# Attention moved to the end of the scan, wide products throughout, and the turn between batches written out by hand, in a fused Mamba and transformer kernel on one core

## The reference

```python
# 1. selective scan over ctx (512 x 256), gated by the normalised x
u = silu(causal_conv4(in_proj @ ctx.T) + conv_b)          # 512 channels x 512 tokens
dt = softplus(dt_proj @ (x_proj[:16] @ u) + dt_b);  Bm, Cm = x_proj[16:] @ u
state = state * exp(dt * A) + dt * u * Bm                  # 16 states per channel
y = sum_n(state[n] * Cm[n]) + D * u
x = x + tanh(g0) * (y * silu(layernorm(x))).T
# 2. feed-forward with weights rounded to -1, 0, 1 and activations rounded to 8 bits
x = x + tanh(f0) * bitlinear(gelu(bitlinear(layernorm(x), w1)), w2)
# 3. attention over features: energies of ctx, applied to the normalised x
x = x + tanh(g1) * layernorm(x) @ softmax(q(ctx) @ k(ctx).T).T
# 4. ordinary feed-forward in float32, 512 -> 2048 -> 512
x = x + tanh(f1) * (gelu(layernorm(x) @ p1.T + b1) @ p2.T + b2)
```

## Time and profile before

| | |
|---|---|
| device time, median of 3 runs | 1057.2 us (1055.8 to 1058.83) |
| the profiled execution | 1057.6 us, its span 1055.8 us |
| busy share of the span | PE 78%, DVE 78%, ACT 63%, POOL 53% |
| granted TensorE clock, mean | 0.896 |
| chain that ended last, by engine | PE 27%, DVE 21%, issue 17%, ACT 13%, DMA 9%, POOL 8% |
| the same scans of the last two loop passes | start at 601.42 and 833.70 us |
| closing part begins on TensorE | 911.52 us |

### The profile page before, as it was taken

One profiled execution on the slowest core, in us unless ns is written; L12 is line 12 of the kernel. 1 busy time (PEld: TensorE's weight loads), 2 busy tenths in 40 slices (PEclk: granted clock), 3 DMA queues, 4 the chain that ended last, 5 costly groups with the idle time before them and its releaser, 6 DMA issues.

```text
span 1055.8 us, 10904 instructions
## 1 busy us (share of the span) xinstructions
PE 823.3 (78%) x2704; PEld 399.7 (38%) x2704; DVE 824.9 (78%) x1001; ACT 665.5 (63%) x972; POOL 564.1 (53%) x493
## 2 busy tenths in 40 slices
PE   5442320699699987989699988889799988898998
PEld 2110110344334334444334334344333434445887
DVE  4879968887988897687998898777998897764333
ACT  4679969366589962365589962565599852533442
POOL 0398785123997783123997783134997782133000
PEclk9555555799899999998999999998999999999999
DMA  7069985001199897201199897201298995200222
GB/s 276 0 119 205 231 195 107 0 1 41 22 190 206 189 251 179 77 26 40 20 198 201 191 246 179 102 0 40 50 204 184 203 219 155 99 1 21 94 90 76
DMA packets 51439, 130.07 MB, mean 123 GB/s; under 512 B 6304, under 2 KB 7456, under 8 KB 50864
## 3 DMA queue, kind: packets, MB, share of 16 engines
q0 software_dynamic: 17280, 62.92, 32.4%
q1 hardware_dynamic: 34096, 66.53, 18.6%
HBM read 62.33 MB, written 4.19 MB: 63 GB/s over the span
## 4 chain that ended last, share of the span: by engine, by line
PE 27%; DVE 21%; issue 17%; ACT 13%; DMA 9%; POOL 8%; DVEq 1%; ACTq 0%; POOLq 0%
DMA u<-work 9%; DVE pair L1194 7%; PE bank L630 4%; PE pair L514 4%; PE pair L630 4%; POOL work L1600 4%; PE bank L615 3%; DVE pair L1207 3%; PE pair L542 3%; ACT pair L825 2%; ACT L825 2%; PE bank L602 2%; ACT L1074 2%; PE pair L591 1%; POOL u L1611 1%
## 5 line engine op out<-in xcount | busy, mean ns | idle before, releaser
L1600 POOL TENSOR_TENSOR work<-du,bcast 128x1024 f32<-128x1024 f32 x128 | 346.8, 2736 | 54.0 <-DVE du L1256 45.6
L825 ACT ACTIVATE pair<-dt,a_neg 128x512 f32<-128x512 f32 x256 | 166.3, 683 | 63.3 <-DVE work L1199 52.6
L1194 DVE TENSOR_TENSOR_SCAN pair<-pair,work 128x512 f32<-128x512 f32 x160 | 186.9, 1214 | 16.3 <-ACT pair L825 15.7
L602 PE MATMUL bank<-stage,ring 128*128 128x512 f32 x384 | 174.8, 598 | 11.0 <-ACT stage L1074 3.7
L1611 POOL DMA_DIRECT2D u<-work x120 | 126.0, 1050 | 67.6 <-DVE work L1211 22.4
L423 PE MATMUL bank<-xd,pick 128*128 128x512 bf16 x128 | 56.9, 445 | 101.9 <-ACT bcast L810 66.1
L1207 DVE TENSOR_TENSOR_SCAN pair<-pair,work 128x512 f32<-128x512 f32 x96 | 117.4, 1223 | 18.1 <-ACT pair L825 17.7
L602 PEld LDWEIGHTS bank<-stage,ring 128*128 128x128 f32 x384 | 70.4, 189 | 96.4 <-issue 78.5
L1199 DVE TENSOR_TENSOR work<-pair,ccast 128x1024 f32<-128x1024 f32 x80 | 98.0, 1225 | 11.4 <-DVE pair L1194 6.1
L615 PE MATMUL bank<-ring,stage 128*128 128x512 f32 x192 | 88.8, 614 | 8.4 <-DVE stage L1476 7.0
L423 PEld LDWEIGHTS bank<-xd,pick 128*128 128x128 bf16 x128 | 13.1, 103 | 161.7 <-ACT bcast L810 101.0
(11 more groups left out here) (181 smaller groups left out, 1606.9 us busy)
## 6 DMA issues: line engine op xcount, KB each, us to landing
u<-work POOLq DMA_DIRECT2D x120, 512.0 KB, 5.7
ring<-ffn_dram SPq DMA_DIRECT2D x144, 256.0 KB, 5.0
ring<-ffn_dram SPq DMA_DIRECT2D x16, 512.0 KB, 3.3
xres<-x_dram SPq DMA_DIRECT2D x4, 1024.0 KB, 5.2
stage<-w_dram SPq DMA_DIRECT2D x1, 4096.0 KB, 17.4
stage<-w_dram SPq DMA_DIRECT2D x4, 1024.0 KB, 6.8
out_dram<-stage SPq DMA_DIRECT2D x16, 256.0 KB, 2.1
ctxT<-ctxT_dram SPq DMA_DIRECT2D x4, 512.0 KB, 6.4
```

The lines of the kernel that those rows point to most:

```text
L602: last = pe.matmul(banks[2 + f % 2][:], piece(f)[:, k * P:(k + 1) * P], xnT[:, k, :], start=k == 0, stop=k == J - 1)
L825: act.activation(pairs[s % DECAYBUFS][:, q, :], dt[:, p * HALF + q, :], ACT.Exp, scale=a_neg[:, p * HALF + q, n:n + 1]).then_inc(s_decay, 1)
L1194: dve.tensor_tensor_scan(pair[:, q, :], pair[:, q, :], rows[:, q, :], 0.0, ALU.mult, ALU.add).then_inc(s_scan, 1)
L1600: pool.tensor_tensor(work[:, s % SCANBUFS, :, :], du[:, p * HALF:(p + 1) * HALF, :], bcast[:, n % 2, :].unsqueeze(1).broadcast_to([P, HALF ...
```

## The change

- `SLOTS` becomes 13. Slots 13 and 14 disappear; each engine gets a function `turning` (in the first pass `first_turning`) with the same work written out in a new order.
- Attention moves from slots 6 to 9 to slots 9 to 12. Its last transposes and copy stand behind the scan.
- Every half step is wide; the narrow form is gone.
- `FFN_DOWN` puts a fourth pair into slot 9, so 13 pairs stand in the scan instead of 12, and the other three in the turn: one ahead of the gate's transposes, two behind them.
- The rounding's multiplication (scale, plus a constant that rounds) goes from VectorE to ScalarE (`q_scale`), and its row buffer x1n becomes two.
- The mean for the gate goes from GpSimd to ScalarE (`gate_mean`).
- In `between` and `closing` a few neighbours trade places: on VectorE `second` of tiles 1 and 2 comes one step earlier, on GpSimd `norm` before `h_round`, on TensorE the first broadcast before the first attention product, on ScalarE three copies ahead of two others.

```diff
-SLOTS = 15
+SLOTS = 13
-ATT_SLOTS = {6: 0, 7: 1, 8: 2, 9: 3}
-ATT_LAST_SLOT = 10
+ATT_SLOTS = {9: 0, 10: 1, 11: 2, 12: 3}
-FFN_DOWN = {(9, 0): (0, 0), (9, 1): (0, 2), (9, 3): (0, 4),
-            (10, 0): (0, 6), (10, 1): (0, 8), (10, 3): (0, 10),
...
+FFN_DOWN = {(9, 0): (0, 0), (9, 1): (0, 2), (9, 2): (0, 4), (9, 3): (0, 6), (10, 0): (0, 8), (10, 1): (0, 10), (10, 3): (0, 12), (11, 0): (0, 14), (11, 1): (1, 0), (11, 3): (1, 2), (12, 0): (1, 4), (12, 1): (1, 6), (12, 3): (1, 8)}
-FOURTH_SLOTS = {(11, 0): 0, (14, 1): 1}
+FOURTH_SLOTS = {(11, 0): 0}
-        x1n = ccast[:, 0, :]
+        x1n = ccast
```

TensorE behind slot 12:

```diff
+            def turning(b, m):
+                f_pair(b, 1, 10)
+                gate_transposes(m, (0,))
+                gate_transposes(m, (1,))
+                gate_transposes(m, (2,))
+                f_pair(b, 1, 12)
+                f_pair(b, 1, 14)
+                q_transposes(m, (0,))
+                gate_transposes(m, (3,))
                 up1(m, 0, range(FC - 1))
-                if prev is not None:
-                    f_unit(prev, QUANT_SLOT, 0)
                 up1(m, 0, (FC - 1,))
                 q_transposes(m, (1,))
...
+                att_transpose(m, J - 1)
+                if rest:
+                    turning(b, m)
```

ScalarE:

```diff
+            def gate_mean(b, j):
+                act.wait_ge(s_zsum, b * J + j + 1)
+                act.activation(zst[:, j, 1:2], zst[:, j, 0:1], ACT.Copy, scale=-1.0 / D).then_inc(s_zmean, 1)
+            def q_scale(b, t):
+                act.wait_ge(s_q1s, b * T + t + 1)
+                act.activation(x1n[:, t % 2, :], x1n[:, t % 2, :], ACT.Identity, scale=mst[:, t, 12:13],
+                               bias=expo[:, 2:3]).then_inc(s_q1m, 1)
+            def turning(m):
+                q_scale(m, 0)
                 q_copy(m, (0,))
+                q_scale(m, 1)
+                gelu1(m, 0, range(FC - 2))
+                gelu1(m, 0, range(FC - 2, FC))
                 q_copy(m, (1,))
+                q_scale(m, 2)
+                q_scale(m, 3)
```

VectorE, where the narrow form of `half_step` goes and the turn is written out:

```diff
-                for q in range(HALF):
...
-                    dve.tensor_tensor(row, state, ccast[:, n % 2, :], ALU.mult).then_inc(s_hc, 1)
+            def turning(b, m):
+                last_sum(m, 0)
+                last_sum(m, 1)
+                gated(m, 0)
+                gated(m, 1)
+                first_sum(m, 0)
+                first_sum(m, 1)
+                q_norm(m, 0)
+                q_norm(m, 1)
+                q_out(m, 0)
+                first_sum(m, 2)
+                first_sum(m, 3)
+                q_norm(m, 2)
+                q_out(m, 1)
+                q_norm(m, 3)
+                q_out(m, 2)
+                fourth(b, 1)
+                q_out(m, 3)
```

GpSimd:

```diff
-                if slot == ZSTAT_SLOT - 1:
-                    for j in range(J):
...
-                        pool.tensor_scalar(zst[:, j, 1:2], zst[:, j, 0:1], -1.0 / D, 1.0, ALU.mult,
-                                           ALU.mult).then_inc(s_zmean, 1)
```

179 lines of the change are left out of this document (90 added, 89 removed), and 4 rows, old and new, of the table FFN_DOWN.

## The result

The changed kernel takes 1029.97 us (median of 4 runs, 1028.3 to 1030.91) where the one before takes 1056.5 us (1052.77 to 1058.83): the ratio is 0.975, with a 95% interval of 0.9725 to 0.9775. It is faster, and 1 us from the forecast of 1029. Its profiled execution took 1030.36 us, with a span of 1028.5 us.

What follows compares the result with a forecast made beforehand. No single engine bounds it: VectorE and ScalarE stand in a ring holding the attention. Loop passes -6.3 + 1.0 - 3.6 = -8.9, three times -26.7; first pass -1, closing -0.4: 1057.6 to 1029.5, median 1029 us; range 1014 to 1047.

Steps and rivals of the forecast that it cites:

- Slots 5 to 8: Loop passes' scan: with attention moved out, 15.2 us a slot, 60.8 instead of 68.7 us, so 7.9 us less.
- about a microsecond: ScalarE in slots of 15.2 us: slack left between a product's end and the time it comes to that pair.
- The wide form: Scan products of slots 5 to 8 as one wide instruction instead of narrow ones: costed at nothing.
- its rival: Slots 5 to 8: wide products make decays late, slots 16.5 instead of 15.2 us, 1045 us in all; chance 0.16.
- Slots 9 to 12: Loop passes' scan, taking the attention: slots of 16.0, 15.6 and 16.5 us, then 7.35 us to the last product.
- Behind the last product: End of the scan: the gate ends 8.4 us behind the last product instead of 7.4, so 1.0 us more.
- The turn: From the gate's end to the next pass's start: 19.3 instead of 22.9 us, so 3.6 us less a pass.
- TensorE reaches its transposes at +8.5: After the gate's end: TensorE transposes the first rounded row 8.5 us later, behind three transposes and two pairs of down units.
- First pass: Before the loop passes: mean wait goes, statistics wait grows, attention shifts cost; sum about -1 us, between -5 and +4.
- The stretch between the passes: Code of `between`: neighbours that trade places cost nothing; if a cover is gone, 2 us either way a pass.
- The DMA rival: Scan: accumulating DMAs become the bound, landings of 8.6 us give 1068 us, slower than before; chance 0.08.
- state of 7.5 us: Scan: 116.3 / 15.5 = 7.5 us a state, denser than 7.9 before, which a DMA landing must not exceed.

Runs made afterwards that it cites:

- the experiment: Changed kernel with only the first pass's attention put back in slots 6 to 9, loop passes as they are: 1024.99 us, ratio 0.9701 against the kernel before.

## Why the prediction was right, and where it was off

**Slots 5 to 8** (4 x 15.2 = 60.8 forecast): 15.64 + 46.66 = 62.3 us in the third pass, and 62.9 in the two others with their longer slot 5. The mechanism is shown: put back, the attention makes slots of 17.7. The step that was mis-sized is "about a microsecond" of slack on ScalarE with a period of 7.31. The period is 7.77. I had subtracted the scaling of 0.72 from 8.03, a half slot in which ScalarE did not wait for an up unit. Now it waits 0.25 us for the second one, and 0.2 us more lie between its instructions, which overlap less. The sum took each engine by itself, and the ring through both is longer.

**The wide form** at nothing, and its rival at 1.3 us a slot: nothing, shown from both sides.

**Slots 9 to 12**: 15.69, 15.21 and 16.49, and 7.34 to the last product, against 16.0, 15.6, 16.5 and 7.35. Good to 0.4 us each. The rows of slots with and without a maximum were enough for it. The scan from slot 5 is 117.0 us against 116.3.

**Behind the last product**: 7.87 us against 8.4 forecast. The kernel before took 7.36 in the one pass I had read, but 8.81 and 8.55 in the two others, where its last sums waited longer for DMAs. So the new block is 0.5 us longer than in that pass, where 1.0 was forecast, and yet 1.1 us shorter over three. I had carried one pass over to three.

**The turn**: from the gate's end 21.3 against 19.3. The step that failed is "TensorE reaches its transposes at +8.5": the count of what stands between the transposes and the rounded row was right, but I let TensorE begin at the gate's end and left out that `f_pair(b, 1, 10)` and the last transposition stand before it, on an engine that is behind from slot 11; it reached them at +10.1. I had costed the two sums of `fourth` on VectorE, but not asked when TensorE's next pair is released by them. With the lateness gone the 19.3 are there: 19.3, 19.5 and 19.1 us with the attention early and this very turn, 19.3 and 19.1 with `fourth` early. Over three passes the gain is 9.6 all the same, since the other two turns of the kernel before were 25.9 and 24.4 us, not the 22.9 of the pass that I had read. That is 4.4 us of luck: in those two the clock had dropped, in the changed kernel's three it had not. At a full clock on both sides the turn gained 22.9 - 21.2 = 1.7 us a pass, less than half of the 3.6 forecast.

**First pass**: +3.5 against -1, inside my bounds of -5 to +4. The direction of each piece was right (the wait for the mean was replaced by one for the statistics), but the attention beside w2's quantisation was under-sized: I gave it 2.8 us in slots 10 to 12 and 0.6 behind them, and the experiment shows 1.9 and 3.2 in slots 10 and 11, 0.3 in slot 9, and 2.2 behind. These are good to about 1 us: slot 10 of the first pass took 23.1 to 24.3 us in the kernels that share its code.

**The stretch between the passes**: -5.5 where I said nothing. The swaps are worth nothing, or 0.5 us a pass under a drop. What changed is where TensorE's clock fell, and I had not looked at the granted clock of the kernel before in that stretch.

**The DMA rival**, to which I gave 0.08, is nearer than that: its sign is right for the version with the attention in its old place, and the attention itself, by making the slots longer, keeps it away. Its state of 7.5 us was mis-counted too: slots 5 to 12 hold 15 states, not 15.5, so 116.3 us are 7.8 each.

The errors are +4.5, -5.5, +2.7, -4.1, +1.2 and +1.8 us, and add to 0.6, with 0.3 for the start. A forecast that is 1 us from the result with terms off by 5 was lucky in its sum, if not in its mechanisms. How lucky, the clock shows: 5.5 us in the stretch and 4.4 in the turns came from where it dropped, and 1.3 in slot 5 and up to 1.4 in the closing went the other way. By these numbers I estimate 1037 us for the changed kernel with the drops of the kernel before.

## What to carry to other kernels

A wait that two engines can pay should be paid by the one with slack: `fourth` at the end of slot 10 turned TensorE's wait of 3.57 us into one of 2.73 us on VectorE and made the kernel slower; one half step later, with TensorE's pairs moved ahead of it, neither waits, and the kernel is the fastest of all. Costing a stretch from one pass of several is only as good as that pass; read the same stretch in all of them, and the granted clock with it, before putting a number on a loop. A bound can be a ring through two engines, longer than the work of either: follow who waits for whom once around. And an edit that is right for a loop can be wrong for its first pass, where other work stands beside it: here that alone was worth 5 us.
